# Attention in a one-core transformer block: how far maxima run ahead of scores, and where heads and maxima are transposed in a step

## The reference, cut to what matters

```python
inner = (x @ Wi).reshape(Bb, Tt, Hh, dh).transpose(0, 2, 1, 3)      # 16 heads of 8
outer = (x @ Wo).reshape(Bb, Tt, Hh, dh).transpose(0, 2, 1, 3)
alignment = jnp.einsum('bhqd,bhkd->bhqk', inner, outer) / scale
attn_align = jax.nn.softmax(alignment, axis=-1)
attn = attn_align * aperture.transpose(0, 2, 1)[..., :, None] * expression.transpose(0, 2, 1)[..., None, :]
attn = attn / (attn.sum(axis=-1, keepdims=True) + 1e-08)
v = (x @ Wv).reshape(Bb, Tt, Hh, dh).transpose(0, 2, 1, 3)
converged = jnp.einsum('bhqk,bhkd->bhqd', attn, v)
...
return combined @ Wout
```

## Time and profile before

| | us |
|---|---|
| median of three runs | 482.74 (482.29 to 483.13) |
| the profiled execution | 482.52 |
| span of its trace | 480.8 |
| PE busy | 397.7 (83%) |
| DVE busy | 385.2 (80%) |
| ACT busy | 232.2 (48%) |
| granted TensorE clock, mean share of full speed | 0.933 |

### The profile page before, as it was taken

The page is one execution under the profiler, slowest core; times in us unless marked ns, Lnnn a source line. Parts: engine busy times, 40 slices in busy tenths (PEclk is TensorE's granted clock), DMA queues, the critical chain, the costliest instruction groups (busy, mean ns, idle before and its releaser), DMA issues.

```text
span 480.8 us, 7695 instructions
## 1 busy us (share of the span) xinstructions
PE 397.7 (83%) x2204; PEld 213.2 (44%) x2204; DVE 385.2 (80%) x841; ACT 232.2 (48%) x439; POOL 54.5 (11%) x103
## 2 busy tenths in 40 slices
PE   2702999999778889999999999999977019999995
PEld 1600456776543543333333333334427004567764
DVE  6698957788789888999898899987546889577883
ACT  2400453432341157777777777778863003543322
POOL 4520002122000010000000000000014400011210
PEclk9999999999897669999999999999996558999998
DMA  6100002223069721111112111100200000022103
GB/s 178 46 0 0 1 1 67 65 58 92 4 237 287 274 79 46 45 46 46 44 49 56 60 49 52 44 1 2 67 1 0 0 1 1 1 65 65 41 25 89
DMA packets 25767, 27.48 MB, mean 57 GB/s; under 512 B 3920, under 2 KB 17488, under 8 KB 25680
## 3 DMA queue, kind: packets, MB, share of 16 engines
q1 hardware_dynamic: 25744, 27.20, 18.6%
HBM read 17.08 MB, written 9.98 MB: 56 GB/s over the span
## 4 chain that ended last, share of the span: by engine, by line
PE 64%; DVE 16%; issue 12%; ACT 4%; POOL 1%; DMA 1%; DVEq 0%; ACTq 0%; POOLq 0%
PE ps L1151 14%; PE ps L1161 13%; PE ps L1136 6%; PE ps L1038 5%; DVE probs L748 4%; DVE neg_max L810 3%; PE ps L1021 3%; PE ps L1053 3%; PE ps L1023 3%; PE ps L1054 3%; PE ps L1022 3%; ACT probs L599 2%; PE ps L963 2%; PE ps L1170 2%; DVE heads_out L709 2%
## 5 line engine op out<-in xcount | busy, mean ns | idle before, releaser
L810 DVE TENSOR_REDUCE neg_max<-ps 128x1 f32<-128x512 f32 x256 | 161.1, 681 | 14.3 <-PE ps L1136 14.2
L599 ACT ACTIVATE probs<-ps 128x512 f32<-128x512 f32 x256 | 136.8, 601 | 44.0 <-PE ps L1151 42.8
L1136 PE MATMUL ps<-stacks 63*128 63x512 f32 x256 | 105.7, 494 | 3.3 <-DVE neg_max L810 2.6
L1151 PE MATMUL ps<-stacks 64*128 64x512 f32 x256 | 95.0, 462 | 4.9 <-ACT probs L599 4.8
L1151 PEld LDWEIGHTS ps<-stacks 64*128 64x128 f32 x256 | 41.3, 190 | 76.3 <-ACT probs L599 65.7
L1161 PE MATMUL ps<-probs,v_ext 128*32 128x512 f32 x512 | 69.0, 612 | 0.0
L1136 PEld LDWEIGHTS ps<-stacks 63*128 63x128 f32 x256 | 43.8, 196 | 19.5 <-DVE neg_max L810 15.0
L525 ACT CAST stacks<-ps 128x512 fp32r<-128x512 f32 x32 | 17.2, 588 | 67.5 <-PE ps L1002 67.5
L771 DVE TENSOR_TENSOR vae_and_gates<-heads_out,ps 128x512 f32<-128x512 f32 x32 | 21.9, 686 | 21.3 <-ACT heads_out L533 19.3
L453 POOL TENSOR_TENSOR w_lo<-w_gu,w_hi 128x512 fp32r<-128x512 f32 x16 | 20.6, 1295 | 150.1 <-ACT w_hi L512 150.1
L748 DVE TENSOR_TENSOR probs<-slot_row,slot 128x1024 f16<-128x1024 f16 x32 | 36.5, 1219 | 0.1
(11 more groups left out here) (150 smaller groups left out, 539.2 us busy)
## 6 DMA issues: line engine op xcount, KB each, us to landing
stacks<-parts_dram SPq DMA_DIRECT2D x64, 128.0 KB, 2.4
parts_dram<-part_hi SPq DMA_DIRECT2D x8, 512.0 KB, 3.5
parts_dram<-part_lo SPq DMA_DIRECT2D x8, 512.0 KB, 5.8
w_gu<-in_L_ffn_Wg_dram SPq DMA_DIRECT2D x16, 128.0 KB, 2.1
w_gu<-in_L_ffn_Wu_dram SPq DMA_DIRECT2D x16, 128.0 KB, 2.2
wd_sb<-in_L_ffn_Wd_dram SPq DMA_DIRECT2D x16, 128.0 KB, 2.2
x<-in_L_attn_x_dram SPq DMA_DIRECT2D x4, 256.0 KB, 3.7
stacks<-k_rows_dram SPq DMA_DIRECT2D x2, 512.0 KB, 6.6
```

The lines of the kernel that those rows point to most:

```text
L599: nc.scalar.activation(probs[:, u // HG, u % HG, :], ps[:, RING + ring_bank(step, u), :], ACT.Exp, scale=SCORE_SCALE).then_inc(probs_ready, 1)
L810: nc.vector.tensor_reduce(neg_max[:, g, col, qt:qt + 1], ps[:, ring_bank(step, u), :], AX.X, ALU.max, negate=True).then_inc(max_taken, 1)
L1136: nc.tensor.matmul(ps[:, ring_bank(step, u), :], q_stack[rows, g, pp, chunk(qt)], k_stack[rows, g, pp, :], start=True, stop=True).then_inc ...
L1151: nc.tensor.matmul(ps[:, RING + ring_bank(step, u), :], k_stack[rows, g, pp, chunk(c)], q_stack[rows, g, pp, :], start=True, stop=True).th ...
```

## The change

Numbers of a step are n, units u from 0 to 15.

- The maximum products beside step n are now the late half (units 8 to 15) of step n + 1, and then the early half (0 to 7) of step n + 2 (`units_beside`), in place of all 16 of step n + 2.
- Ahead of step 0, PE and DVE handle the maxima of step 0 and the early half of step 1. The late half of step 1 moves into step 0, and in the end eight maxima of step 15 stand in step 14, which had none.
- The heads are transposed at k = 2 and not at k = 4; the maxima of step n + 1 at k = 4 and not at k = 0, and now behind the norm of the heads of step n - 1. ACT's copy of the maxima moves from behind its third exponential to behind its eleventh.
- DVE begins the norm after its sixth reduction of a step, not the ninth.
- The wait for the stacks of step n + 2 moves from the step's start to k = 4.
- In steps 14 and 15 the transposes of combined heads and the projections are at other places (`TURN_COMBINED_AT`, `PROJECT_AT`), and DVE's order there follows.

```diff
--- before.py
+++ after.py
@@ -262,13 +262,21 @@
 
             return u // HG, (u + 1) % HG
 
-        def ring_wait(n, step, u, first_step):
-
-
-            return n * MAX_UNITS + (u + 1 + (RING - 1 if step == first_step and u == 0 else 0))
+        def ring_wait(n, step, u, first_step, first=0):
+
+
+            return n * MAX_UNITS + (u + 1 + (RING - 1 if step == first_step and u == first else 0))
         TURN_BANK, OUT_BANK = (0, 0, 0, 4), (1, 1, 1, 5)
-        HEADS_AT, TURN_AT = 3, 4
-        NORM_AT = 9
+        HEADS_AT, TURN_AT, TURN_MAX_AT = 3, 2, 4
+        NORM_AT = 6
+        LATE = MAX_UNITS // 2
+        TURN_COMBINED_AT = {(2, 5): 0, (3, 0): 1, (3, 4): 2}
+        PROJECT_AT = {(2, 7): 0, (3, 2): 1, (3, 6): 2}
+
+        def units_beside(n, step, late=True, early=True):
+
+            return ([(n + 1, step + 1, u) for u in range(LATE, MAX_UNITS)] if late else []) + (
+                [(n + 2, step + 2, u) for u in range(LATE)] if early else [])
 
         def after(i, o, per, more=0):
 
@@ -598,7 +606,7 @@
                         act.wait_ge(probs_used, n * C + (u // HG + 1))
                     nc.scalar.activation(probs[:, u // HG, u % HG, :], ps[:, RING + ring_bank(step, u), :],
                                          ACT.Exp, scale=SCORE_SCALE).then_inc(probs_ready, 1)
-                    if u == 2 and has_next:
+                    if u == 2 * TURN_MAX_AT + 2 and has_next:
                         copy_max_rows(n + 1, (g + 1) % 2)
                     if u == HEADS_AT and has_before:
                         copy_heads(n - 1, (g - 1) % 2)
@@ -859,7 +867,6 @@
             split_qk_lo(3)
             take_maxima(1, range(MAX_UNITS // 2))
             add_bias(3)
-            take_maxima(1, range(MAX_UNITS // 2, MAX_UNITS))
             dve.wait_ge(gate_exp_ready, 1)
             nc.vector.tensor_scalar(gate_one, gate_exp, 1.0, None, ALU.add).then_inc(gate_one_ready, 1)
             dve.wait_ge(gate_one_ready, 1)
@@ -886,27 +893,27 @@
                 nc.vector.tensor_tensor(dst, o[:, :, :, 0:DH], den_r[:].unsqueeze(3).broadcast_to([P, C, HG, DH]),
                                         ALU.mult).then_inc(heads_normed, 1)
 
-            def attend(b, step, steps, has_max):
+            def attend(b, step, steps, early=True):
 
                 n = b * G + step
-                units = iter(range(MAX_UNITS) if has_max else ())
+                units = iter(units_beside(n, step, early=early))
 
                 def take(count):
                     for _ in range(count):
-                        u = next(units, None)
-                        if u is not None:
-                            take_max(n + 2, step + 2, u)
+                        unit = next(units, None)
+                        if unit is not None:
+                            take_max(*unit)
 
                 take(NORM_AT)
                 if step > 0:
                     norm_heads(b, step - 1, steps, lambda: take(1))
                 take(MAX_UNITS)
 
-            attend(0, 0, None, True)
+            attend(0, 0, None)
             with dve.Fori(0, B - 1) as b:
                 steps = Steps(dve, dve_heads, b, 3 * G)
                 for step in range(1, G + 1):
-                    attend(b, step, steps, True)
+                    attend(b, step, steps)
                 steps.end_turn()
 
             def copy_combined(b):
@@ -923,15 +930,15 @@
 
             steps = Steps(dve, dve_heads, B - 1, 3 * G)
             norm_steps = Steps(dve, dve_norm[2])
-            attend(B - 1, 1, steps, True)
+            attend(B - 1, 1, steps)
+            attend(B - 1, 2, steps, early=False)
             copy_combined(0)
             add_attention(0)
             copy_combined(1)
-            norm_heads(B - 1, 1, steps)
             add_attention(1)
+            norm_heads(B - 1, 2, steps)
             copy_combined(2)
             add_attention(2)
-            norm_heads(B - 1, 2, steps)
             norm_apply(2, 0, norm_steps)
             norm_heads(B - 1, 3, steps)
             copy_combined(3)
@@ -1132,7 +1139,7 @@
                 g = step % G
                 qt, j = max_unit(u)
                 rows, pp = slice(TILE * (j % 2), TILE * (j % 2) + MAX_ROW), j // 2
-                pe.wait_ge(max_taken, ring_wait(n, step, u, 3))
+                pe.wait_ge(max_taken, ring_wait(n, step, u, 2, LATE))
                 nc.tensor.matmul(ps[:, ring_bank(step, u), :], q_stack[rows, g, pp, chunk(qt)], k_stack[rows, g, pp, :],
                                  start=True, stop=True).then_inc(max_scores_ready, 1)
 
@@ -1174,33 +1181,35 @@
 
                 g, n = step % G, b * G + step
                 pe.wait_ge(max_rows_loaded[g], (b + step // G) * 32 + 32)
-                has_max = not last_batch or step < 2
-                if has_max:
-                    pe.wait_ge(stacks_loaded[(g + 2) % G], (b + (step + 2) // G) * STACK_DMAS + STACK_DMAS)
-                has_next = not last_batch or step < G - 1
+                late, early = not last_batch or step < G - 1, not last_batch or step < 2
+                has_next = late
+                units = iter(units_beside(n, step, late, early))
+
+                def max_product():
+                    unit = next(units, None)
+                    if unit is not None:
+                        max_scores(*unit)
+
                 for k in range(MAX_UNITS // 2):
+                    if k == LATE // 2 and early:
+                        pe.wait_ge(stacks_loaded[(g + 2) % G], (b + (step + 2) // G) * STACK_DMAS + STACK_DMAS)
 
                     scores(n, step, 2 * k)
-                    if has_max:
-                        max_scores(n + 2, step + 2, 2 * k)
+                    max_product()
                     scores(n, step, 2 * k + 1)
-                    if has_max:
-                        max_scores(n + 2, step + 2, 2 * k + 1)
-                    if k == 0 and has_next:
-                        turn_max(n + 1, (g + 1) % G, None if first else n)
-                    if last_batch and step > 1:
-
-                        done = 2 * (step - 2) + k // 4
-                        if k % 4 == 0 and done < B - 1:
-                            turn_combined(done)
-                        if k % 4 == 2 and done < B - 1:
-                            project_out(done)
+                    max_product()
+                    if not first and k == TURN_AT:
+                        turn_heads(n - 1, g - 1, n + 1)
+                    if k == TURN_MAX_AT and has_next:
+                        turn_max(n + 1, (g + 1) % G, None if first else n + 1)
+                    if last_batch and (step, k) in TURN_COMBINED_AT:
+                        turn_combined(TURN_COMBINED_AT[step, k])
+                    if last_batch and (step, k) in PROJECT_AT:
+                        project_out(PROJECT_AT[step, k])
                     if k == 1 and not first:
                         products(n - 1, (g - 1) % G, C - 1)
                     if k in (3, 5, 7):
                         products(n, g, k // 2 - 1)
-                    if not first and k == TURN_AT:
-                        turn_heads(n - 1, g - 1, n + (2 if has_next else 1))
 
             def first_maxima(n, units):
                 pe.wait_ge(stacks_loaded[n], STACK_DMAS)
@@ -1216,7 +1225,6 @@
             turn_max(0, 0, None)
             first_maxima(1, range(MAX_UNITS // 2))
             project_vae(3)
-            first_maxima(1, range(MAX_UNITS // 2, MAX_UNITS))
             pe.wait_ge(vae_ready, 2 * B)
             pe.wait_ge(qk_lo_ready, 2 * B)
             attend(0, 0, first=True)
```

## The result

| | before | after |
|---|---|---|
| median of the runs, us | 482.51 (4 runs, 481.76 to 483.13) | 488.69 (4 runs, 486.92 to 489.76) |
| ratio, 95% interval | | 1.0125 (1.009 to 1.016) |
| profiled execution, us | 482.52 | 489.13 |
| span of its trace, us | 480.8 | 487.4 |

The changed kernel is slower by 6.2 us. The two spans differ by 6.6.

What follows compares the result with a forecast made beforehand. PE was taken as bound by a loop of waits per quarter, DVE as the bound ahead of step 0. Terms -4.2 + 5.6 + 2.7 = +4.1 gave 486.6, plus 0.2 carried over 486.8 us, range 484.1 to 488.6.

Steps and rivals of the forecast that it cites:

- Part 1: Ahead of step 0: with eight maxima gone, gates wait only for ACT's exponential and start earlier; gain 4.2 us, 3.8 to 5.1.
- The rival of the clock's earlier return: Step 0: earlier dense work brings the 2.4 GHz clock sooner, gain 5.1 us, total 485.9; chance 0.15.
- the bound on the other side: Step 0: the low clock level reaches a score pair further into the work, up to 0.4 us less gain.
- Part 2: Steps 1 to 13: moved transposes and norm change the quarters by +0.26, +0.40, -0.23 and 0; +5.6 us, 4.5 to 6.5.
- the term from M8's product to TM: Quarter of s8: ninth maximum product, its reduction, the norm's product, then semaphore; the transpose of maxima goes at 1.44 us.
- The bound of 0.50 a step: Steps 1 to 13: upper bound of the added time per step, forecast at +0.43 us, lower bound 0.35.
- The rival that TM's wait is covered: Quarter of s8: norm ends early enough to hide the transpose of maxima; 2.77 us, total 479.3; chance 0.10.
- Part 3: Steps 14 and 15: added maxima and transposes or projections outside the wait for the first exponential cost +2.7 us, 2.0 to 3.2.
- The last term, +0.55: Step 15, quarter of s12: the projection delays the last two exponentials, before ACT's square roots for the norm; +0.55 us.
- The rows of maxima: Step starts: rival that maxima's rows land late, beyond the 4.65 us available; total 488 to 490; chance 0.05.

Runs made afterwards that it cites:

- b_turn2: Kernel of before with heads transposed at k = 2, not 4, and the norm begun behind the sixth reduction, not the ninth: 481.22 us, ratio 0.9968.
- e_ahead: Changed kernel with the late half of step 1's maxima again computed and reduced ahead of the gates: 494.2 us.
- e_tm5: Changed kernel with maxima transposed at k = 5, not 4, and copied behind the thirteenth exponential: 500.8 us.
- e_norm5: Changed kernel with the head norm begun behind the fifth reduction of a step, not the sixth: 482.10 us, ratio to before 0.9982.
- e_norm7: Changed kernel with the head norm begun behind the seventh reduction of a step, not the sixth: 508.9 us.
- e_ends: Changed kernel with step 14's first transposes of combined heads at k = 4, not 5, and first projection at k = 6, not 7: 487.8 us.
- e_swap: Changed kernel with heads transposed at k = 6, after the maxima at k = 4, norm behind the fourteenth reduction, step 14's places earlier: 478.70 us, ratio to before 0.9927.

## Why the prediction was right, and where it was short

The forecast was slower, 486.8, in a range up to 488.6; the median is 488.69, just above the range. By the profiled executions the sum was +4.1 and the traces differ by 6.6.

| part | forecast | traces |
|---|---|---|
| up to the start of step 1 | -4.2 | -4.4 |
| steps 1 to 13 | +5.6 | +7.5 |
| step 14 | +1.3 | +1.3 |
| step 15 | +1.4 | +1.3 |
| behind the last exponential | 0 | +1.0 |

**Part 1** has its mechanism right: the gates wait for ACT only. That its 4.2 fits the 4.4 so well is in part luck. The 4.4 contains 0.5 by which the last bias came earlier in this execution (162.99 against 163.46), and it lost 0.3 by the clock: the quarter of s8 of step 0 took 3.25 (172.28 to 175.53), where it took 2.96 in before. From the last bias to the start of step 1 the old order takes 19.2 us in before, 18.9 in b_turn2 and 19.2 in e_ahead; the new one takes 14.7 to 15.3 in seven traces (e_tm5, which waits for rows there, left out). So the part is worth 3.6 to 4.5, and the cause is shown by e_ahead.

The clock did not move with the work. In before it was 0.50 from 150.4, rose at about 163.8, fell again at about 167.3 and stayed low until 177.4. In the changed kernel it did not rise in between, and P of step 0 still took 1.86. Here are before and then the changed kernel:

```profile
150.40:163.60 13.20, 11.69 (x26) 6.35 (x27) 12.09 (x21) 1.54 (x2) 0.00 (x0) 0.50 0.67 221
164.00:167.00 3.00, 2.16 (x7) 0.73 (x4) 2.90 (x5) 0.61 (x1) 0.00 (x0) 1.00 1.02 376
```

```profile
150.40:174.00 23.60, 20.05 (x55) 10.24 (x56) 20.01 (x34) 7.52 (x13) 2.06 (x8) 0.50 0.69 231
```

The rival of the clock's earlier return gave nothing: the clock did return 3.4 us earlier, but the work from M3 on had moved by 4.7 (167.31 against 172.03), and P of step 0 still ran ahead of the return. What came is the bound on the other side, the low level reaching a score pair further (0.3 of the 0.4 allowed). Nor is the place fixed: in e_norm5, whose program is the same up to step 1, the clock returned at about 173.0 and the quarter behind it took 2.74. The rule that stood with that rival (the Trainium skill, TensorE: Matmul & The Clock Gate, Part 1, What's actually happening: activity releases the throttle) is in agreement with the direction, since the dense work began earlier and the return came earlier; it says nothing of whether the work gains by it, and here it did not.

**Part 2** has its mechanism and its quarters right, 3.04 (3.03), 2.77 (2.76), 2.77 (2.78), and one of them short: the quarter of s8 with 3.32 forecast and 3.46 measured. The step that failed is the term from M8's product to TM, 1.44. Its first piece was right, 0.57 for 0.56. From the reduction to the norm's product it was 0.61 and not 0.54: I took the row of a reduction that started directly behind the reciprocal and lasted 0.63, and M8's starts out of idle time and lasts 0.69, as the first row of that group does. From the end of the norm's product to TM it was 0.14 and not 0.06. In e_norm5 the same interval is 0.14 again, with the norm's product 0.54 behind a reduction in a row. Why it is 0.14 stays open. That PE must load weights behind the signal does not explain it: in before the same product of the norm ends at 359.19 and the transposes of combined heads, which load weights too, go at 359.25. 0.15 a step over 13 steps is 1.9 us, all of the difference in the second row of the table. The bound of 0.50 a step was too narrow for it (it was 0.58). The first piece could have been read from before; for the second I know of no row there.

**The wait is the norm and not the late half's reductions**: e_norm5 and e_norm7 moved it down and up as the walk says, and no other part of the kernel was touched. The rival that TM's wait is covered falls with them.

**Part 3** holds piece by piece: step 14 was forecast with quarters of 2.77, 3.04, 3.17, 3.70 and has 2.74, 3.03, 3.19, 3.69. Step 15's second was 3.82 and has 3.68: the projection's first matmul follows the heads' transpose in 0.49 and the next score follows that in 0.99, each a little less than the terms I took. The last term, +0.55, came out as 0.57, but its terms as written, 0.43 + 1.09 + 0.53 and two exponentials against 1.19 and one and a half, give about 1.2: that it fits is luck, or a slip in writing it down. e_ends shows that a projection's cost is its place.

**The rows of maxima**: not late in the changed kernel, and e_tm5 shows how near it is.

**The last row of the table** I had not priced. Nothing shows it to be the change's: e_norm5, e_ends and e_norm7 have 126.8 to 127.1 there, before 126.4. See the last section.

**What the change was worth by parts.** Ahead of step 0 it gains about 4; turning the heads early is a gain of its own, 1.8 us over steps 1 to 13 (b_turn2). Both are lost to one order, maxima behind heads in the bank that they share: 0.7 a step from 2.77 to 3.47 in the quarter of s8, 9 us in all. Steps 14 and 15 cost 2.6 more. Turned round (e_swap), with the places of e_ends, the kernel keeps the gain ahead of step 0, its steps cost about what they did in before, and its ratio to before is 0.9927, some 3.5 us faster.

## What to carry to other kernels

Where PE runs in a ring with another engine, look for the one stretch of a round in which it waits anyway: what stands in it is free, and what stands one instruction outside costs all of its length. Before a wait is moved later in an engine's order, follow what it waits for back through the other engine's order; here a transpose came to wait for an operation that stood behind a reduction of a product that the same quarter had just issued. Price such a chain from rows in the same state as it will have (an operation behind idle time, the same pair of instructions at a wait), since small errors come 13 times.

## What the runs showed of the hardware that I had not expected

**Waits of 1.56 us in a busy stretch went with a lower clock.** In the changed kernel, with 0.87 us of waiting for the norm and PE busy for 10.53 of a step's 12.03 us, the granted clock stayed at 2.4 GHz through 13 steps. With 1.56 us (e_norm7) it fell to 1.2 GHz once a step in nine of 13, and doubled what the longer wait cost; in the other four the same wait left it at 2.4 GHz. In e_tm5, with its wait of 1.0 to 1.1 us at a step's start, it fell in three steps of 13. What decides it in a single step no run here shows.

**The stretch of low clock behind the attention differs between executions.** From its last exponential to its end the work is the same in all eleven traces, and took from 126.4 to 128.3 us. The two longest, b_turn2 and e_ahead, are the two with the longest stretch at the lower clock there, 44 us; in before it was 34 us and in the changed kernel 41. These are the two stretches, of before and then of the changed kernel; the first begins 10.8 us behind the last exponential and the second 5.3:

```profile
365.20:399.20 34.00, 11.09 (x45) 7.29 (x44) 26.12 (x76) 3.79 (x6) 8.66 (x16) 0.50 0.00 0
```

```profile
365.30:406.10 40.80, 17.07 (x70) 12.30 (x69) 31.42 (x97) 4.67 (x8) 10.61 (x19) 0.50 0.00 0
```

The 1.0 us in the last row of the table lies within what the timed runs of one kernel spread (486.9 to 489.8), and no experiment here ties it to the change. It is why the quarters of a step tell more here than the total time.
